# The store of each radial-embedding piece moved from group 14 + 7i to group 18 + 7i of SyncE's first pass

## What is computed

```python
# layer 0
alpha = sum(q[dst] * k[src], -1) / sqrt(32)         # 4 heads
e = exp(alpha - segment_max(alpha, dst)[dst])
out = segment_sum(e / segment_sum(e, dst)[dst] * v[src], dst) + x @ Wskip.T + bskip
# ... Wout, layer norm, MLP 128-512-128, layer norm; x = layernorm(x + out4)
# layer 1, r = edge_weight
emb = exp(-0.5 * ((clip(r, 0, 1) - centers) * 7) ** 2) * sqrt(8) * (r <= 1)   # (E, 8)
w = silu(silu(emb @ w0 + b0) @ w1 + b1) @ w2 + b2                             # (E, 4, 32)
# messages from w, the features of src and the direction of each edge,
# summed over dst, two output products; x = layernorm(x + ...)
```

## Time and profile before

| | |
|---|---|
| median of the runs | 2978.21 us |
| the profiled execution, its span | 2979.6 us |
| first pass, about | 50 to 1490 us |
| node stage between the passes | 1490 to 1610 us |
| second pass and end | 1610 to 2980 us |
| PE busy over the span | 1851.9 us (62%) |
| DVE busy | 1673.9 us (56%) |
| POOL busy | 1569.1 us (53%) |
| ACT busy | 1271.8 us (43%) |

### The profile page before, as it was taken

The page is one execution under the profiler, slowest core; times in us unless marked ns, Lnnn a source line. Parts: engine busy times, 40 slices in busy tenths (PEclk is TensorE's granted clock), DMA queues, the critical chain, the costliest instruction groups (busy, mean ns, idle before and its releaser), DMA issues. The chain is left out here.

```text
span 2979.6 us, 37370 instructions
## 1 busy us (share of the span) xinstructions
PE 1851.9 (62%) x9706; PEld 1441.9 (48%) x9706; DVE 1673.9 (56%) x4970; ACT 1271.8 (43%) x3058; POOL 1569.1 (53%) x1617
## 2 busy tenths in 40 slices
PE   3255454454554554454568177778787887887787
PEld 2244344354443444444555055555555555555556
DVE  2355555555554555554666055666656655666668
ACT  0245444455454555454545033434334334334345
POOL 4345455555555555555302756666666666666640
PEclk7556666656666666666678577888888778888889
DMA  6456454545555555544301211111111111111110
GB/s 213 135 140 170 134 136 133 138 135 144 142 137 137 140 143 138 145 130 134 109 2 35 53 39 43 45 47 44 45 45 44 45 44 44 44 44 46 46 36 24
DMA packets 242944, 271.84 MB, mean 91 GB/s; under 512 B 46236, under 2 KB 201970, under 8 KB 242220
## 3 DMA queue, kind: packets, MB, share of 16 engines
q0 software_dynamic: 64480, 158.57, 19.7%
q1 hardware_dynamic: 178252, 110.87, 13.6%
HBM read 257.11 MB, written 12.15 MB: 90 GB/s over the span
## 5 line engine op out<-in xcount | busy, mean ns | idle before, releaser
L476 POOL DMA_INDIRECT rows<-kv_tab,src_col x806 | 766.9, 951 | 691.5 <-DVE msg L1048 438.6
L490 POOL DMA_INDIRECT rows<-up_tab,src_col x806 | 796.4, 988 | 488.4 <-DVE rows L1362 240.9
L706 PE MATMUL ps<-hotT,rows 128*128 128x128 f32 x3232 | 511.1, 324 | 314.5 <-DVE rows L1369 164.5
L706 PEld LDWEIGHTS ps<-hotT,rows 128*128 128x128 f32 x3232 | 486.6, 235 | 365.4 <-DVE rows L1369 191.0
L524 PE MATMUL ps<-qwin,hotT 128*128 128x128 f32 x1616 | 357.4, 384 | 404.9 <-issue 194.5
L1333 DVE TENSOR_TENSOR acc<-acc,ps 128x256 f32 x808 | 338.1, 418 | 352.3 <-remote 207.1
L524 PEld LDWEIGHTS ps<-qwin,hotT 128*128 128x128 f32 x1616 | 320.1, 289 | 432.0 <-issue 335.7
L1065 DVE TENSOR_TENSOR acc<-acc,ps 128x128 f32 x808 | 228.0, 282 | 421.8 <-remote 329.4
L533 PE MATMUL ps<-hots,msg 128*128 128x128 f32 x1616 | 334.2, 373 | 48.9 <-DVE msg L1048 28.8
L533 PEld LDWEIGHTS ps<-hots,msg 128*128 128x128 f32 x1616 | 294.5, 273 | 81.3 <-DVE msg L1048 49.3
L757 ACT ACTIVATE hotT<-rel,consts 128x512 f32<-128x512 bf16 x202 | 145.0, 718 | 418.0 <-DMA qwin<-q_tab 303.6
(11 more groups left out here) (169 smaller groups left out, 2192.2 us busy)
## 6 DMA issues: line engine op xcount, KB each, us to landing
qwin<-q_tab SPq DMA_DIRECT2D x808, 64.0 KB
rel<-rel_far SPq DMA_DIRECT2D x202, 128.0 KB
rows<-kv_tab,src_col POOLq DMA_INDIRECT x806
rows<-up_tab,src_col POOLq DMA_INDIRECT x806
rows<-emb_rows SPq DMA_DIRECT2D x202, 16.0 KB
weights<-r_far SPq DMA_DIRECT2D x25, 128.0 KB
emb_rows<-weights SPq DMA_DIRECT2D x25, 128.0 KB
kv_tab<-rows SPq DMA_DIRECT2D x12, 256.0 KB, 2.8
```

The costliest lines, as they stand in the source:

```text
L476: nc.gpsimd.indirect_dma_start(kvr[:, q % RING, k, :], None, kv_tab, bass.IndirectOffsetOnAxis(src_col[:, t:t + 1].bitcast(U32), 0)).then_ ...
L490: nc.gpsimd.indirect_dma_start(upr[:, q % RING, k, :], None, up_tab, bass.IndirectOffsetOnAxis(src_col[:, t:t + 1].bitcast(U32), 0)).then_ ...
L706: mm = pe.matmul(ps[:, 4 + 2 * (q % 2) + k // 2, (2 * (k % 2) + m) * P:(2 * (k % 2) + m + 1) * P], left[:, q % 2, k, :], hot2[:, q % 2, k, ...
```

## The change

```diff
@@ -425,8 +425,8 @@
-                if emb_step(q, 14) is not None:
-                    store_embedding(emb_step(q, 14))
+                if emb_step(q, 18) is not None:
+                    store_embedding(emb_step(q, 18))
                 if q + 1 in STOPS[1:-1]:
                     batch_rows(STOPS.index(q + 1))
```

## The result

The changed kernel takes 2968.89 us (median of five runs, 2959.30 to 2969.38), the kernel before 2984.41 us over its five runs (2977.77 to 2989.45). The ratio is 0.9946, 95% interval 0.9927 to 0.9964: 16 us faster (11 to 22). The time forecast, 2952 us, was 17 us too low; against the three runs of before that stood at its start (2978.21 us) the gain is 9 us, where 26 had been forecast.

A forecast was written before the change was run, and what follows sets the result against it. The first pass was taken as bound by engines waiting for one another, not by one engine. 2978.2 - 28 (late windows) + 2 (first store) gave 2952 us; own range 2905 to 2963, 8 in 10 up to 2990.

The forecast's parts named there:

- The direction and the removed wait: SP's queue, first pass: the 150.3 us of waits for the exponential ahead of stores fall to nearly nothing; kernel faster.
- Waits at L375: SP's waits for its permission, `qe_ready`, in the first pass: up from 29.4 us to 100 us or more.
- POOL's wait for messages: POOL's waits for DVE's messages in the first pass, 357.3 us: down by about 20 us.
- I take half of 57 us: 28 us: First-pass gain: PE's wait for late `hotT`, 47.6 us scaled to 57, halved as one of two followed cases was on the path.
- the forecast's own range: Whole kernel's time: 2905 to 2963 us, given a chance of 0.55.
- Rival A: First pass: slow stretches with POOL's gather bursts set the pace; 2978 us less 0 to 10; chance 0.27.
- slow stretches: First-pass stretches where DVE stands still and SP issues slowly while POOL gathers without a break; said to be there regardless of stores.
- Rival B: First pass: SP, no longer held, adds traffic where POOL gathers; 22 us slower, 3000 us; chance 0.17.
- The new neighbours: Spread of piece i + 2 now two groups behind the store, not six; its buffer free, 0 as a rule.
- the 2 us term: Added once for the first store, now behind the 1600 KB load of `x_rows` at group 18, possibly landing late.
- the bound in the prediction: First store landing only behind the 1600 KB load: 11.7 us less 6.8 us of SP's issue, 5 us, once.
- unchanged within 3 us: Sign for the second pass, which the change does not touch: its time stays within 3 us.

The follow-up runs named there:

- e5: The changed kernel itself, all 26 stores moved, against the kernel before on a slow chip: 3008.40 us, ratio 0.9937.
- e11: Only the stores of pieces 0 to 4 at 18 + 7i, others at 14 + 7i, against the kernel before on a slow chip: 3014.33 us, 0.9961.
- e6: The kernel before, unchanged, one run for its trace, on a slow chip where the kernel before takes 3026 to 3028 us.
- e12: Only the stores of pieces 5 to 25 at 18 + 7i, against the kernel before on a slow chip: 3014.12 us, 0.9956.
- e9: Kernel before with two of four gathers per group from group 16 on, first pass, against the kernel before, slow chip: 2553.27 us, 0.8445.
- e10: Changed kernel with the same halved gathers in the first pass, against the kernel before, slow chip: 2513.55 us, 0.8322.
- e2: Only the stores of pieces 5 to 25 at 18 + 7i, against the kernel before on a quick chip: 2238.42 us, 0.9986.
- e16: The changed kernel itself, all stores moved, against the kernel before on a quick chip: 2236.63 us, 0.9995.
- e7: Changed kernel with half the bytes per first-pass gather from group 16 on, against the kernel before, slow chip: 3010.35 us, 0.9953.

## Why the prediction was half right

**The direction and the removed wait: right.** L402's wait is gone. Waits at L375 are 313 us (forecast: 100 or more), ACT's for windows 31 us (about 100), PE's for `hotT` none (under 20). POOL's wait for messages fell by 14 us (about 20).

**"I take half of 57 us: 28 us": mis-sized.** This is the term that failed. The 57 us were a count of how long PE waited for a late `hotT`, and they did go. But to halve them on two cases was no measure of the path. In its place the runs show 16 us here and 19 in e5, and 9 against the three runs at which the forecast began; 2969 us lies above the forecast's own range, 2905 to 2963, and inside the one to 2990. And it isn't made of even pieces: the forecast comes to 1.1 us a store, measured were 2.4 us for each of the first five and 0.6 us for each of the others. I had scaled a rate read from 200 to 1400 us to the whole pass, which leaves out the first store. In the traces with it moved (after, e5, e11) the product of group 16 comes at 182 to 184 us, in those without (before, e6, e12) at 187 to 189, so this one alone gives 3 to 7 us; and the later ones I overrated. That the two errors partly cancel in the sum is luck.

What I had not priced is the overlap. That POOL's gathers hide most of the later waits is shown by e9 and e10, where half of them gone makes the same move worth 40 us. How it goes on in single groups is my reading: a late window is paid for only when PE and DVE could have gone on, and ACT's second condition, `qe_ready`, takes up most of what the windows give back: 220.0 us "remote" where 65.1 stood.

**Rival A: a large part of what happened.** In the steady course the slow stretches absorb most of it: ACT's wait for windows fell by 168 us and DVE's remote waits grew by 9. I gave it 0.27 and "0 to 10 us" by this mechanism; the measured 16 us lie between it and the forecast, and e12's 9 to 18 us for the later stores alone stand at its upper end or above. e9 shows that the standstills come with POOL's gathers, e10 against e9 that with half of the gathers the move gives 40 us.

**Rival B: did not happen.** DVE's remote waits are 319.9 against 310.9 us and the groups behind 24 were 7 us faster, not 50 slower. From e6 to e5 they are 4 us slower with 25 us more of remote waits; a few us of B's kind can't be told from the scatter of traces.

**The new neighbours: right, and the 2 us term can be seen.** No wait of L396 for the landing of a store appears in the list of SP after: there SP issued the first store at 174.27 us and reached the spread at 184.60. On a quick chip SP is faster, and every trace there with the first store moved and four gathers a group has one such wait, 1.9 to 2.7 us; e2, with the store at its old place, has none. In e16 it is at group 20, behind the 1600 KB load (its wait, then SP's timeline):

```profile
SPq L396 <- DMA emb_rows<-weights: 2.1, 1, 2.1
...
113.41 0.42 SPq L421 DMA_DIRECT2D acc<-in_x_rows  x1
113.89 0.57 SPq L402 DMA_DIRECT2D emb_rows<-weights  x1
...
125.09 0.59 SPq L396 DMA_DIRECT2D weights<-r_far  x1
```

The spread went out 11.2 us behind the store, where the median store of that trace landed after 3.7 us; the load landed after 10.4. So this store did land late, about with the load, as the bound in the prediction had it. Whether it stood behind the load in order or merely shared the DMA engines with it isn't told apart. It cost the kernel nothing that shows.

**Second pass "unchanged within 3 us": 4.4 us longer in this pair** (1493.1 and 1497.5), 1.1 us in e6 and e5 (1496.5 and 1497.6). I take it for the scatter of single traces, for which I had left too little room.

## What to carry to other kernels

Taking a long wait off a queue shortens a kernel only where nothing slower runs beside it. Before a wait is priced, compare the period of a group with the issue time of the slowest engine (here 4 x 1.25 us); where they meet, as in e16, the price is near zero. List every condition of the instruction that waits, as the next one takes over when the first is met in time (`qe_ready` here). Read the first batches apart from the steady course, since what binds later has not begun there. And take the hiding work away once (here half of the gathers): the 97 us against 1 us told in one pair what the waits themselves could not.

## What the runs showed of the hardware that I had not expected

The same program takes 2237 us in one group of runs and 3028 us in another, with the same busy time of DVE (1666 us in e16, 1672 us in e5). PE's is 1693 and 1845 us, at a mean granted clock of 0.84 and 0.73. Of the 773 us between these two spans, 453 lie up to the last product of the first pass (at 1055.5 and 1508.0 us), and there the difference goes with standing still beside long rows of GpSimd's indirect gathers. The other 321 us lie behind it, where the gathers of the second pass run, and no run here touches them. On the slow chips DVE and PE work on for about 6 us beside such a row and then stop until it ends; two gathers per group instead of four gave 475 us back there and 92 us on a quick chip. Half the bytes per gather gave nothing on a slow one (e7). What differs between the two groups was not found: whether it is the chip, the lower clock, or something else is open, and so is why DVE and PE stop.
